# One-hots of the second stage wait for the loop part of the preceding bucket, with a wider 16-bit bucket table

## The reference, cut to what matters

```python
def _L0_gnn_ref(h, edge_index, edge_attr, W1, b1, W2, b2, gamma, beta, eps_gin):
    src, dst = (edge_index[0], edge_index[1])
    agg = jax.ops.segment_sum(h[src], dst, num_segments=N)
    z = (1.0 + eps_gin) * h + agg
    z = jax.nn.relu(z @ W1 + b1) @ W2 + b2
    mean = jnp.mean(z, axis=0)
    var = jnp.var(z, axis=0)
    z = (z - mean) * jax.lax.rsqrt(var + BN_EPS) * gamma + beta
    return z + h

def _L1_gnn_ref(x, edge_row, edge_col, edge_val, weight):
    gathered = edge_val[:, None] * x[edge_col]
    support = jax.ops.segment_sum(gathered, edge_row, num_segments=N_NODES)
    return jax.nn.relu(support @ weight)

x = _layernorm(x + _L0_gnn_ref(x, edge_index, ...), axis=-1)
x = _layernorm(x + _L1_gnn_ref(x, src, dst, edge_weight, L1_gnn_weight), axis=-1)
```

## Time and profile before

| | us |
|---|---|
| median of 3 runs | 5424.88 (5422.3 to 5427.39) |
| span of the profiled execution | 5351.1 |
| outside the span | 73.8 |
| first stage, first tile to last | 65 to 2700 |
| between the stages (batch norm, layer norm) | about 2700 to 2970 |
| second stage | about 2970 to 5351 |

### The profile page before, as it was taken

One profiled execution on the slowest core, in us unless ns is written; L12 is line 12 of the kernel. 1 busy time (PEld: TensorE's weight loads), 2 busy tenths in 40 slices (PEclk: granted clock), 3 DMA queues, 4 the chain that ended last, 5 costly groups with the idle time before them and its releaser, 6 DMA issues.

```text
span 5351.1 us, 79415 instructions
## 1 busy us (share of the span) xinstructions
PE 3721.5 (70%) x16131; PEld 3045.6 (57%) x16132; DVE 2301.2 (43%) x5448; ACT 1495.5 (28%) x4377; POOL 3177.6 (59%) x3352
## 2 busy tenths in 40 slices
PE   2677676667667776767742667777777777777777
PEld 2565555555555655656632556566665666665666
DVE  2545454545555544545563233333333333333333
ACT  2444444445444444444552000000000000000001
POOL 6666655565656665666335666666666666666662
PEclk6887888888887878888855789888888888888898
DMA  4333333333333333333293333333333333333331
GB/s 134 93 97 92 99 90 97 90 97 93 95 93 97 93 97 91 96 97 99 62 298 123 90 94 99 96 101 96 100 101 99 95 100 100 102 97 97 100 100 53
DMA packets 298112, 541.14 MB, mean 101 GB/s; under 512 B 77802, under 2 KB 190302, under 8 KB 297838
## 3 DMA queue, kind: packets, MB, share of 16 engines
q0 software_dynamic: 159424, 434.52, 28.3%
q10 hardware_dynamic: 89348, 67.77, 4.0%
q1 hardware_dynamic: 49066, 36.39, 2.2%
HBM read 489.80 MB, written 46.88 MB: 100 GB/s over the span
## 4 chain that ended last, share of the span: by engine, by line
issue 27%; ACTq 16%; another core or an unknown queue 15%; PE 15%; ACT 12%; DVE 9%; DVEq 4%; DMA 2%; SPq 1%; POOL 0%; PEldq 0%; POOLq 0%
PE ps L1419 10%; ACT ones_sb L1613 7%; DVE work L1096 7%; ACTq L1611 4%; ACTq L1613 2%; DVEq L1096 2%; PE ps L1221 2%; ACT ring L1611 2%; ACTq L1642 1%; PE ps L1459 1%; ACT ones_sb L1619 1%; ACTq L1617 1%; ACTq L377 1%; PE ps L1292 1%
## 5 line engine op out<-in xcount | busy, mean ns | idle before, releaser
L548 POOL DMA_INDIRECT ring<-in_x,idx x1664 | 1587.9, 954 | 1039.5 <-issue 456.4
L606 POOL DMA_INDIRECT ring<-x_dram,idx x1612 | 1528.0, 948 | 904.9 <-issue 479.8
L1419 PE MATMUL ps<-ring,work 128*128 x6448 | 1631.3, 411 | 581.1 <-DVE work L1096 387.5
L1419 PEld LDWEIGHTS ps<-ring,work 128*128 128x128 f32 x6448 | 1327.7, 208 | 851.0 <-issue 649.4
L1221 PE MATMUL ps<-ring,ones_sb 128*128 x3708 | 1115.7, 449 | 454.8 <-ACT ones_sb L1619 301.9
L1096 DVE TENSOR_SCALAR work<-ps,dstT,wT 128x256 f32<-128x256 f32 x1612 | 748.0, 536 | 1551.6 <-remote 977.0
L1221 PEld LDWEIGHTS ps<-ring,ones_sb 128*128 128x128 f32 x3708 | 800.4, 225 | 676.6 <-issue 550.2
L1613 ACT ACTIVATE ones_sb<-tile_nodes,dstT 128x128 f32<-128x128 f32 x1854 | 651.0, 391 | 396.5 <-issue 331.1
L1292 PE MATMUL ps<-work 128*128 128x128 f32 x3384 | 499.2, 301 | 203.6 <-issue 148.1
L1292 PEld LDWEIGHTS ps<-work 128*128 128x128 f32 x3384 | 484.0, 216 | 233.5 <-issue 189.8
L1791 ACT ACTIVATE work<-ps 128x512 f32<-128x512 f32 x49 | 29.3, 597 | 1764.2 <-remote 1111.7
(11 more groups left out here) (240 smaller groups left out, 2299.3 us busy)
## 6 DMA issues: line engine op xcount, KB each, us to landing
ring<-in_x,idx POOLq DMA_INDIRECT x1664
ring<-x_dram,idx POOLq DMA_INDIRECT x1612
z_dram<-z_pair ACTq DMA_DIRECT2D x49, 256.0 KB
ones_sb<-x_dram ACTq DMA_DIRECT2D x49, 256.0 KB
ring<-z_dram SPq DMA_DIRECT2D x24, 512.0 KB, 4.1
ring<-in_x SPq DMA_DIRECT2D x24, 512.0 KB, 5.6
x_dram<-ring ACTq DMA_DIRECT2D x24, 512.0 KB
out<-ones_sb ACTq DMA_DIRECT2D x48, 256.0 KB
```

The costliest lines, as they stand in the source:

```text
L548: nc.gpsimd.indirect_dma_start(out=ring[:, q, c, :], out_offset=None, in_=x, in_offset=bass.IndirectOffsetOnAxis(ap=idx[:, q, c:c + 1], ax ...
L606: nc.gpsimd.indirect_dma_start(out=ring[:, q, c, :], out_offset=None, in_=x1_dram, in_offset=bass.IndirectOffsetOnAxis(ap=idx[:, q, c:c + ...
L1419: last = nc.tensor.matmul(to[:, t * D:(t + 1) * D], ones_of[:, b, c, t * P:(t + 1) * P], ring[:, ds((p + b) & (RING - 1), 1), c, :].rearra ...
```

## The change

Three things are edited. In the second stage DVE makes the one-hots of a bucket's first four pairs ahead of the loop, behind one wait for the pairs up to `head` of the preceding bucket (whose loop buffers are then free); the loop begins with the fifth pair. For this the bucket table has a sixth column, `PREV2`, with the preceding bucket's `head`, and all its columns are uint16. PE loads six columns too and does not use the sixth. In the first stage `entry` no longer gives a reason to skip the check of the ten loaded values.

```diff
-        table2 = sb("table2", [1, NBK, 5], i32)
+        table2 = sb("table2", [1, NBK, 6], mybir.dt.uint16)
...
         def entry(eng, j):
             _, values = nc.values_load_multi_w_load_instructions(
-                table[0:1, ds(j, 1), :].rearrange("a t f -> a (t f)"), engines=[eng.engine], min_val=0, max_val=MOST,
-                skip_runtime_bounds_check_because=IN_RANGE)
+                table[0:1, ds(j, 1), :].rearrange("a t f -> a (t f)"), engines=[eng.engine], min_val=0, max_val=MOST)
             return values
...
-        NEW2, M42, HEAD2, M22, END2 = range(5)
+        NEW2, M42, HEAD2, M22, END2, PREV2 = range(6)
...
                 setup(nc.vector.tensor_copy(table2[0:1, :, HEAD2], first_pair[0:1, 0:NBK]))
+                setup(nc.vector.memset(table2[0:1, 0:1, PREV2], 0))
+                setup(nc.vector.tensor_copy(table2[0:1, 1:NBK, PREV2], first_pair[0:1, 0:NBK - 1]))
...
             def steps2(j):
-                new, m4, head, m2, end = entry2(dve, j)
+                new, m4, head, m2, end, prev_head = entry2(dve, j)
...
                 with dve.If(new < m4):
-                    with dve.Fori(new, m4, 2 * TWO) as p:
+                    dve.wait_ge(s_added2, prev_head + RING)
+                    stand(dve)
+                    for b in range(0, 2 * TWO, TWO):
+                        weighted(loop2[:, b:b + TWO], new + b, TWO)
+                with dve.If(new + 2 * TWO < m4):
+                    with dve.Fori(new + 2 * TWO, m4, 2 * TWO) as p:
                         for b in range(0, 2 * TWO, TWO):
                             dve.wait_ge(s_added2, p + (b + RING - TWO))
                             weighted(loop2[:, b:b + TWO], p + b, TWO)
...
             def sum_bucket(j, bank, others):
-                new, m4, head, m2, end = entry2(pe, j)
+                new, m4, head, m2, end, _ = entry2(pe, j)
```

## The result

The changed kernel takes 5633.5 us (median of 4 runs, 5620.1 to 5636.8) beside 5423.6 us of the kernel before in the same measurement: a ratio of 1.0394, 95% interval 1.0366 to 1.0422. Forecast were 5510 us in a range from 5300 to 5720. The profiled execution took 5620.1 us, 5618.3 of it span. Every execution whose span is listed takes 1.8 to 3.1 us more than its span, so the profiled execution of the kernel before, with a span of 5351.1 us, took some 5353, 1.3% less than its median. The 73.8 us that were counted as time around its span are mostly this difference.

What follows compares the result with a forecast made beforehand. The prediction took chains of engines as the bound: ACT with its sequencer in the first stage, late-released DVE and POOL's gathers in the second. 5424.9 + 215 (checks) - 130 (one-hots) + 0 (table) = 5510 us, range 5300 to 5720.

Steps and rivals of the forecast that it cites:

- the second rival: Second stage gains nothing, late counts meeting the third wait; first-stage checks cost 215 to 304 us: 5665 us, chance 0.15.
- the signs that the prediction set for being right: First-stage tiles some 2 us longer, more ACT issue idle, PE's one-hot waits 4 to 5 us a bucket, first eight one-hots earlier.
- The one-hots, forecast 130 us gained: Second stage: moving DVE's first four pairs' one-hots gains 2.7 us a bucket, 130 us over 49, range 40 to 230.
- half of the 7.6 us for the first two waits: Second stage: of PE's 7.6 us a bucket idle for DVE's one-hots, replacing DVE's first two waits saves 3.8 us.
- The bound below, nothing: Second stage: lowest gain from the moved one-hots, zero if the whole wait moves to DVE's third wait.
- The checks, forecast 215 us: First stage: ten checked values on PE and ACT add 2.2 us a tile, 215 us over 98 tiles, range 0 to 440.
- If one in six is slow, 1.9 us on top: First stage, ACT: 20 added instructions a tile; if one in six meets a 0.70 us step, 1.9 us more.
- Less the 1.4 us that ACT waits for others: First stage: ACT's 1.4 us a tile of waiting for other engines is subtracted from the checks' cost.
- PE's own 2.6 us fall mostly beside ACT's; its waits for ACT, 2.7 us a tile, cover them: First stage: PE's ten checks, 2.6 us a tile, add nothing because PE already waits 2.7 us for ACT.
- The table, forecast 0: Bucket table's sixth column and 16-bit width, 49 loads each on PE and DVE: 0 us, range -24 to +12.
- The first rival: First-stage checks nearly free, lying under queued work as the sequencer runs ahead, so the change is faster: 5295 us, chance 0.27.
- Each stage is held by a chain of engines: Both stages: no engine is busy 90% of the time, so waits between engines must say what sets the time.

Runs made afterwards that it cites:

- paced kernel: Changed kernel without its checks, all gathers, POOL pausing for two 128x256 fills after each four gathers in both stages: 5317.1 us, 0.9800 of the kernel before.

## Why the forecast was off

The direction was right, the size was not: 210 us lost where 85 were forecast. It is the second rival that came about, checks near 215 us with nothing from the second stage (5665 us); it had a chance of 0.15. All the signs that the prediction set for being right came true as well: tiles 2.6 us longer, more "issue" time on ACT, PE's waits for one-hots down to 4.7 us a bucket, the one-hots ahead of the diagonal. They watched waits and places, and none of them the length of a bucket.

**The one-hots, forecast 130 us gained, measured 10 and not clear of the scatter.** The step that failed is "half of the 7.6 us for the first two waits", less 1.1 given back at the third. The waits did fall as forecast, and the one-hots do stand ahead of PE's products with the diagonal. But the working took a removed wait for removed time. It had the right row in hand, three engines let go within 0.8 us, and wrote "why the counts come late, these rows don't say"; the sum was then made as if they came late by the place of the wait. They come late with POOL's full stream of gathers, whatever stands first behind them takes the delay, and the step should have given it all back. The 161 us came back as 102 of "issue", 6 of waiting for rows and 40 of busy time. The bound below, nothing, was right.

**The checks, forecast 215 us, measured 187 and 198 in the slow condition and 253 with half the gathers.** (The first stage's 256 us in the first pair of traces hold some of those 57 us.) The length of a check was well bounded: 2.6 us for ten against 2.9. The rest was right in sum and wrong in parts. "If one in six is slow, 1.9 us on top": with hardly a slow step on PE, and a fifth of them left on ACT, the checks cost 2.5 us a tile, more than the 187 / 98 = 1.9 us with all slow steps, so slow steps aren't what makes them dear. "Less the 1.4 us that ACT waits for others": no such slack was found. And "PE's own 2.6 us fall mostly beside ACT's; its waits for ACT, 2.7 us a tile, cover them": PE's checks alone cost 1.0399. Those waits vanished, but in a ring of two engines they had not been slack, only the place where the ring's time was booked. The step that PE's checks lie on the path at the tile's start, before its product with zeros, is missing from the prediction, and the trace of before could have shown it. PE's loads there take 1.08 us on the mean in one tile and 2.39 us in the next, by turns, and the array's idle time before the product with zeros is 0.19 us after the short ones and 0.80 us after the long ones (counted over 47 tiles of either): a longer entry had little cover left.

**The table, forecast 0.** PE's load of a bucket's entry went from 1235 to 1454 ns, 219 ns and so 11 us over 49 buckets, near the upper bound, if all of it lay in the open. That speaks against a load by bytes, which are 12 now for 20 before. The Trainium skill (Runtime: NRT & Kernel Launch, Instruction fetch mechanics) puts a loaded register at about 200 ns. The traces show some 240 on PE for most loads: 1235 / 5, 1454 / 6, and 2389 / 10 for the 16-bit rows of the first stage. But of the ten-column rows of 32 bits every second one takes 1.08 us, 110 ns a register, and the others 2.39. The medians of the earlier trace rows and of the changed kernel, 1194 and 1838 ns, fall between the two kinds and mean little; the means are 1.74 and 1.75, so the checks don't lengthen the load, and ten 16-bit values cost 0.65 us more than ten of 32 bits. Why rows differ by turns, no run tells.

**The first rival,** checks nearly free, is true in the quick condition, though not for the reason given: they take the place of waits for POOL's rows, and aren't hidden by the sequencer's running ahead. The Trainium skill's rule (same page and section) says that fetching instructions is hidden under an issue floor. It doesn't say that issuing them is free, which the prediction made of it, and here the checks' own issue, 0.29 us a value with quick steps, is the cost.

**The view of the bound.** "Each stage is held by a chain of engines" was right for the slow condition. That the very same kernel can be POOL-bound at 4330 us was not in any row of the trace of before, except in the floor of 42 us a bucket that the prediction worked out from them; it is what the quick condition shows, 41.5.

## What to carry to other kernels

When several engines are let go at one moment, ask what held them all before taking a wait off one of them: a wait moved under a common delay is only booked elsewhere, and the test is to remove the suspected source (here half the gathers), not the wait. When you write down what would show a forecast right, name the length of the loop, not only the waits in it. Between two engines that hand buffers round, the waits of one for the other are no slack for work put on either; look instead for the first instruction behind the added work, and how long it waits today. Checked register loads cost 0.3 us a value on an engine that does them, so in a loop over tiles keep them off the engines that set its time; beside an engine that is the bound they cost nothing. And before you take the median of an instruction's durations, look whether it has two kinds.

## What the runs showed of the hardware

- The same kernel took 5375 to 5427 us in some groups of runs and 4330 us in others, 20% less, on one chip both. In the second case hardly a sequencer instruction of the stages took over 0.5 us (4 on PE, ACT and DVE, where 1313 did) and no bucket's copy came late. Within a group it doesn't change.
- In the slow condition an unbroken run of gathers by POOL (1.26 us each) goes with sequencer steps of 0.70 us on PE, ACT and DVE and counts that come 5 us and more late. Half the gathers, or a pause of two fills of 0.32 us, each behind a semaphore, after each four gathers, leaves 1 and 33 slow steps of 281 in the second stage and no copy over 2 us late; one such fill does nothing. In the first stage ACT keeps 124 and 303 of 898. How the gathers do it, and why only in this condition, stays open; that the effect is POOL's issue and not its rows' landing isn't shown apart, only that it isn't their mean rate.
- The paced kernel is 2.0% faster than before in the slow condition; with pauses in the first stage only it is 10.3% slower in the quick one, where the fully paced kernel wasn't run.
- PE's load of ten registers from a 32-bit table takes 1.08 and 2.39 us by turns from row to row; from a 16-bit table always about 2.39, and 1.45 for six. A loaded 16-bit value costs as much as a 32-bit one or more.
- A checked value costs two more sequencer instructions, on PE 146 and 18 ns in the median, 0.29 us with the gaps: 2.9 us for ten.
